# The choice of experts moved from the slots stage into the turns of the first token stage

## The reference, cut to what matters

```python
logits = x @ gate_weight.T
probs = jax.nn.softmax(logits.astype(jnp.float32), axis=-1)
topw, topi = jax.lax.top_k(probs, TOP_K)          # TOP_K = 8 of E = 32
topw = topw / topw.sum(-1, keepdims=True)
...
oh = jax.nn.one_hot(flat_e, E, dtype=jnp.int32)
pos = (jnp.cumsum(oh, axis=0) * oh).sum(-1) - 1   # place of each token in its expert's buffer
buf = jnp.zeros((E, CAPACITY, H), x.dtype).at[flat_e, pos].set(flat_x, mode='drop')
```

## Time and profile before

| | us |
|---|---|
| median of 3 timed runs | 3384.29 |
| the profiled execution, its own time | 3380.68 |
| its span | 3378.9 |
| TensorE busy | 3197.8 (95%) |
| Vector busy | 2735.5 (81%) |
| GpSimd busy | 2081.7 (62%) |
| ACT busy | 1560.9 (46%) |

### The profile page before, as it was taken

One profiled execution on the slowest core, in us unless ns is written; L12 is line 12 of the kernel. 1 busy time (PEld: TensorE's weight loads), 2 busy tenths in 40 slices (PEclk: granted clock), 3 DMA queues, 4 the chain that ended last, 5 costly groups with the idle time before them and its releaser, 6 DMA issues. The chain is left out here.

```text
span 3378.9 us, 55655 instructions
## 1 busy us (share of the span) xinstructions
PE 3197.8 (95%) x17324; PEld 2506.5 (74%) x17324; DVE 2735.5 (81%) x5290; ACT 1560.9 (46%) x5449; POOL 2081.7 (62%) x2335
## 2 busy tenths in 40 slices
PE   7999999999979999999999699999999969999998
PEld 5677777777648888888888577777777757778886
DVE  4788888888677887888887379999999879967775
ACT  1766767667521111111111377777777745321111
POOL 1776666766536777777777477777777753443333
PEclk8999999999979999999999899999999989999999
DMA  7345454454465667676766544555554457730111
GB/s 218 100 137 173 122 166 140 137 174 125 141 174 154 171 169 175 170 166 166 176 164 156 112 128 133 160 163 143 151 172 135 138 164 286 274 103 13 26 13 25
DMA packets 284781, 490.97 MB, mean 145 GB/s; under 512 B 54018, under 2 KB 74818, under 8 KB 283778
## 3 DMA queue, kind: packets, MB, share of 16 engines
q1 hardware_dynamic: 243698, 408.87, 39.6%
q0 software_dynamic: 32256, 77.65, 12.4%
q10 hardware_dynamic: 8592, 1.57, 0.3%
HBM read 250.32 MB, written 136.96 MB: 115 GB/s over the span
## 5 line engine op out<-in xcount | busy, mean ns | idle before, releaser
L915 ACT ACTIVATE c_pr<-ps,t_negmax 128x154 f32<-128x154 f32 x1024 | 385.7, 393 | 180.8 <-DVE t_negmax L684 178.6
L684 DVE TENSOR_REDUCE t_negmax<-ps 128x4 f32<-128x616 f32 x512 | 403.6, 788 | 53.3 <-PE ps L980 52.6
L915 ACT ACTIVATE t_pr<-ps,t_negmax 128x154 f32<-128x154 f32 x1024 | 385.6, 393 | 105.8 <-DVE t_negmax L684 101.4
L707 DVE COPY t_pTm<-ps 128x512 f32<-128x512 f32 x448 | 306.0, 683 | 127.3 <-PE ps L993 123.0
L609 POOL TENSOR_TENSOR t_pr<-t_pr,t_inv 128x512 f32<-128x512 f32 x256 | 275.7, 1077 | 191.0 <-DVE t_inv L699 189.3
L609 POOL TENSOR_TENSOR c_pr<-c_pr,t_inv 128x512 f32<-128x512 f32 x256 | 272.0, 1063 | 196.4 <-DVE t_inv L699 195.0
L980 PE MATMUL ps<-t_kst,t_stack 98*128 98x154 f32 x2048 | 353.0, 291 | 26.3 <-DMA t_stack<-t_q_low 10.1
L980 PEld LDWEIGHTS ps<-t_kst,t_stack 98*128 98x128 f32 x2048 | 279.6, 194 | 38.9 <-issue 17.8
L81 PE MATMUL ps<-e_xT_high,e_wgu_high 128*128 128x512 f32 x768 | 302.4, 394 | 1.4 <-DVE e_xT_low L1508 1.4
L83 PE MATMUL ps<-e_xT_high,e_wgu_low 128*128 128x512 f32 x768 | 299.6, 390 | 0.0
L82 PE MATMUL ps<-e_xT_low,e_wgu_high 128*128 128x512 f32 x768 | 299.4, 390 | 0.0
(11 more groups left out here) (373 smaller groups left out, 9320.9 us busy)
## 6 DMA issues: line engine op xcount, KB each, us to landing
t_stack<-t_q_high SPq DMA_DIRECT2D x1016, 64.0 KB, 2.0
c_wgu_in<-in_gate_upT SPq DMA_DIRECT2D x32, 1536.0 KB, 6.4
t_stack<-t_q_low SPq DMA_DIRECT2D x512, 64.0 KB, 2.0
x_dram<-c_wide_rows SPq DMA_DIRECT2D x32, 1024.0 KB, 7.8
c_wd_in<-in_downT SPq DMA_DIRECT2D x32, 768.0 KB, 4.5
t_xbo<-in_x SPq DMA_DIRECT2D x16, 1024.0 KB, 7.0
xw_dram<-t_z SPq DMA_DIRECT2D x16, 1024.0 KB, 5.3
t_xbo<-x_dram SPq DMA_DIRECT2D x16, 1024.0 KB, 11.0
```

The source lines that it names most:

```text
L684: dve.tensor_reduce(negmax[:, u, :], flat[:, at:at + HG * APART].rearrange("p (h n) -> p h n", h=HG)[:, :, 0:KEYS], AX, ALU.max, negate=Tr ...
L707: dve.tensor_copy(pTm[:, g % 2, :, t * P:(t + 1) * P], ps[:, 4, :].rearrange("p (h n) -> p h n", h=HG)).then_inc(s["pTm"], 1)
L915: op = act.activation(pr[:, u % 4, h, :], flat[:, col:col + KEYS], ACT.Exp, bias=negmax[:, u, h:h + 1], accum_out=total[:, u, h:h + 1])
```

## The change

In the first token stage the two copies behind MAX8 go. One turn later four pieces for that tile stand on Vector's list at positions 8, 13, 18 and 26: `mark` (4 match_replace: the eight largest are overwritten), `pick` (logit minus the largest; the selection as "overwritten differs from the logit"), `step` (step_up, the exponentials times the selection, a copy of the last sub-tile's selection) and `weights` (sum, reciprocal, product). ACT takes the exponential at position 15 (`share_out`). SP stores each tile's weights (`store_weights`) between its load of t_xbo and its store of x. The last tile's pieces follow the last turn. The slots stage loses the whole chain and ACT's store of all weights; TensorE's list begins with the 32 counts and puts the two base matmuls between the key products; Vector empties count banks first and adds the value bias last; GpSimd fills the small part of the table early and does its longest memset (BIG) last. SP waits for 12 made tiles, no longer 13.

```diff
-        LOG = 31
+        LOG, WTS, WEX = 31, (8, 13, 18, 26), 15
...
+            def store_weights(j):
+                sp.wait_ge(s["weighted"], j + 1)
+                sp.dma_start(rows(scr["xw"], j)[:, :, D:XW], weight[:]).then_inc(s["w_stored"], 16)
...
+                if 0 <= i - 3:
+                    store_weights(i - 3)
                 if prev:
...
+            def mark(j):
                 dve.wait_ge(s["top"], j + 1)
-                dve.tensor_copy(c["top8"][:, bass.ds(j * TG * TOPK, TG * TOPK)],
-                                top[:].rearrange("p t k -> p (t k)")).then_inc(s["side_out"], 1)
+                for t in range(TG):
+                    op = dve.match_replace(others[:, t, :], top[:, t, :], logit[:, t, :], LOWEST)
+                op.then_inc(s["others"], 1)
+            def pick(j):
+                dve.wait_ge(s["top"], j + 1)
+                dve.tensor_tensor(share[:], logit[:], top[:, :, 0].unsqueeze(2).to_broadcast([P, TG, E]),
+                                  ALU.subtract).then_inc(s["shifted"], 1)
+                dve.wait_ge(s["others"], j + 1)
+                dve.tensor_tensor(sel[:, 1:1 + TG, :], others[:], logit[:], ALU.not_equal).then_inc(s["picked"], 1)
+            def step(j):
+                dve.wait_ge(s["picked"], j + 1)
+                dve.tensor_tensor(c["step_up"][:, TG * j:TG * j + TG, :], sel[:, 1:1 + TG, :], sel[:, 0:TG, :],
+                                  ALU.subtract).then_inc(s["stepped"], 1)
+                dve.wait_ge(s["shared_out"], j + 1)
+                dve.tensor_tensor(share[:], share[:], sel[:, 1:1 + TG, :], ALU.mult).then_inc(s["chosen"], 1)
+                dve.wait_ge(s["stepped"], j + 2)
+                dve.tensor_copy(sel[:, 0, :], sel[:, TG, :]).then_inc(s["carried"], 1)
+            def weights(j):
+                dve.wait_ge(s["chosen"], j + 1)
+                dve.tensor_reduce(wsum[:], share[:], AX, ALU.add).then_inc(s["summed"], 1)
+                dve.wait_ge(s["summed"], j + 1)
+                dve.reciprocal(wsum[:], wsum[:]).then_inc(s["inverted"], 1)
+                dve.wait_ge(s["inverted"], j + 1)
+                reached(dve, s["w_stored"], 16 * j)
+                dve.tensor_tensor(weight[:], share[:], wsum[:].unsqueeze(2).to_broadcast([P, TG, E]),
+                                  ALU.mult).then_inc(s["weighted"], 1)
             def dot(j, t):
...
+                    if gate and 0 <= j - 1:
+                        for when, piece in zip(WTS, (mark, pick, step, weights)):
+                            if at == when:
+                                piece(j - 1)
...
             unrolled(turn)
+            if gate:
+                for piece in (mark, pick, step, weights):
+                    piece(NG - 1)
...
+            def share_out(j):
+                act.wait_ge(s["shifted"], j + 1)
+                act.activation(share[:], share[:], ACT.Exp).then_inc(s["shared_out"], 1)
...
                         part_out(j)
+                    if at == WEX and gate and 0 <= j - 1:
+                        share_out(j - 1)
...
+            assert n_made[0] == TRI_MADE
+            made(pool.memset(table[:, :, P:LOOK], 0.0))
             made(pool.iota(ramp[:], [[1, NT + 1]], base=0, channel_multiplier=-1, allow_small_or_imprecise_dtypes=True))
...
-            made(pool.memset(table[:, :, P:LOOK], 0.0))
             made(pool.memset(zero[:], 0.0))
+            assert n_made[0] == ZERO_MADE
             made(pool.memset(table[NT:NT + 1, :, 0:P], BIG))
             assert n_made[0] == MADE
...
-            act.wait_ge(s["shifted"], 1)
-            act.activation(prob[:], prob[:], ACT.Exp).then_inc(s["exped"], 1)
-            act.activation(edge[:], edge[:], ACT.Exp).then_inc(s["exped"], 1)
+            for q in range(1, 8, 2):
...
                 act.copy(k["high"][:, two, n, :], k["kf"][:, j % 4]).then_inc(s["khigh"], 1)
-            act.wait_ge(s["weights"], 1)
-            act.dma_start(scr["xw"][0:NTOK, D:XW].rearrange("(t p) e -> p t e", p=P),
-                          prob[:]).then_inc(s["put"], 16)
...
-            logits = c["logits"][:].rearrange("p (t e) -> p t e", e=E)
-            top8 = c["top8"][:].rearrange("p (t k) -> p t k", k=TOPK)
-            link(dve.tensor_tensor(edge[:], top8[:, :, TOPK - 1], top8[:, :, 0], ALU.subtract))
-            dve.tensor_tensor(prob[:], logits, top8[:, :, 0].unsqueeze(2).to_broadcast([P, NT, E]),
-                              ALU.subtract).then_inc(s["shifted"], 1)
-            link(dve.memset(restart[:], 1.0))
-            link(dve.memset(restart[:, :, 0:1], 0.0))
...
             dve.wait_ge(s["falls_mm"], 1)
             dve.tensor_copy(table[:, :, P + 2:LOOK].rearrange("t e w -> t w e"),
                             ps[0:NT + 1, HB + 1, 0:2 * E].rearrange("t (w e) -> t w e", e=E)).then_inc(s["tabled"], 1)
+            dve.wait_ge(s["wv_in"], 32)
+            for n in range(KV_JOBS - 8):
+                value_out(n)
...
-                if e == HB * 4:
-                    pe.wait_ge(s["valued"], KV_JOBS - 8)
-                mm = pe.matmul(ps[0:NT, (HB + e // 4) % 8, (e % 4) * P:(e % 4 + 1) * P], step_up[:, :, e], tri[:],
...
+                mm = pe.matmul(ps[0:NT, (HB + e // 4) % 8, (e % 4) * P:(e % 4 + 1) * P], c["step_up"][:, :, e], tri[:],
                                start=True, stop=True)
                 if e % 4 == 3:
...
+                if j < HB:
+                    return (s["counted1"], 3 + j // 2) if j % 2 else (s["counted0"], 3 + j // 2)
+                return (s["evacuated"], j - HB + 1) if j < 8 + HB else (s["valued"], j - HB - 7)
+            def bases_between(j):
+                if j == 2:
+                    pe.wait_ge(s["made"], TABLE_MADE)
+                    pe.wait_ge(s["counted0"], 4)
+                    pe.wait_ge(s["counted1"], 4)
+                    pe.matmul(ps[0:NT + 1, HB, 0:E], ramp_b[:], table[0:NT, :, P - 1], start=True,
+                              stop=True).then_inc(s["based"], 1)
+                if j == 4:
+                    pe.wait_ge(s["parted"], 1)
+                    pe.matmul(ps[0:NT + 1, HB + 1, 0:2 * E], falls[:], parts[:].rearrange("t w e -> t (w e)"), start=True,
+                              stop=True).then_inc(s["falls_mm"], 1)
+            kv_products(pe, ps, k, s, HB, bank_free, c["key_weights_in"], c["context_in"], bases_between)
```

More of the change, by code:

```diff
@@ L177, with kv_products @@
 KV_JOBS = 13
-def kv_products(pe, ps, k, s, banks, freed, wk_in, ctx_in):
+def kv_products(pe, ps, k, s, banks, freed, wk_in, ctx_in, between=None):
     pe.wait_ge(wk_in, 16)
@@ L185, in kv_products @@
         bank = j % banks
-        if j >= banks:
-            pe.wait_ge(*freed(j - banks))
+        if between:
+            between(j)
+        if freed(j):
+            pe.wait_ge(*freed(j))
         if j == 8:
@@ L738, in logits @@
                 dve.wait_ge(s["side_mm"], j + 1)
[L739 removed]
+                reached(dve, s["picked"], j)
                 dve.tensor_reduce(logit[:], ps[:, T_BANK, :].rearrange("p (t k e) -> p t e k", k=DC, e=E),
@@ L1150, in expert_slots_phase @@
         bkt = sb("bkt", [P, DC, B])
[L1151 to L1154, removed]
         ones, tri = sb("ones", [P, P]), sb("tri", [P, P], BF16)
@@ L1163, in expert_slots_phase @@
         s = Sems(nc, ctx, "r", "wv_in tau_in tail scaled kf khigh matmul evacuated lowered valued stored "
-                               "made shifted exped step weights selected stepped count_mm counted0 counted1 based parted "
+                               "made step count_mm counted0 counted1 based parted "
                                "falls_mm tabled put")
         block = ctx.enter_context(nc.Block())
-        MADE = 13
+        TRI_MADE, TABLE_MADE, ZERO_MADE, MADE = 3, 9, 12, 13
         @block.sync
@@ L1248, in _ @@
                 act.copy(k["high"][:, two, n, :], k["kf"][:, j % 4]).then_inc(s["khigh"], 1)
-            act.wait_ge(s["weights"], 1)
-            act.dma_start(scr["xw"][0:NTOK, D:XW].rearrange("(t p) e -> p t e", p=P),
-                          prob[:]).then_inc(s["put"], 16)
-            for q in range(1, 8, 2):
-                act.wait_ge(s["count_mm"], q + 1)
-                act.copy(table[0:NT, 4 * q:4 * q + 4, 0:P], ps[0:NT, (HB + q) % 8, :].rearrange("t (e n) -> t e n", n=P)).then_inc(
-                    s["counted1"], 1)
         @block.vector
@@ L1307, in _ @@
-            value_out(1)
-            link(dve.reciprocal(ws[:], ws[:]))
-            dve.tensor_tensor(prob[:], prob[:], by_tile(ws), ALU.mult).then_inc(s["weights"], 1)
-            value_out(2)
-            dve.wait_ge(s["made"], MADE)
-            link(dve.memset(table[:, :, P:P + 1], float(P)))
-            link(dve.memset(table[0:1, :, P:P + 1], 0.0))
-            link(dve.memset(table[NT:NT + 1, :, P + 1:P + 2], 1.0))
-            value_out(3)
-            value_out(4)
             for q in range(0, 8, 2):
@@ L1320, in _ @@
```

(13 more changed lines are left out.)

57 lines of the change are left out of this document (21 added, 36 removed).

## The result

| | before | after |
|---|---|---|
| median of 7 timed runs | 3384.29 us | 3393.60 us |
| their range | 3379.73 to 3387.03 | 3388.51 to 3400.38 |
| profiled execution, own time | 3380.68 | 3391.85 |
| its span | 3378.9 | 3390.1 |

The ratio is 1.0031 with a 95% interval of 1.0021 to 1.0041: slower, on the side of the forecast, but 9.3 us between the medians and 11.2 between the profiled executions against the 21 worked out. The forecast median was 3404 us.

What follows compares the result with a forecast made beforehand. TensorE was taken to bound the token stage, with Vector feeding it with little to spare mid-turn. Terms 24.3 + 5.1 - 8.1 gave +21 us, 3402 by the profiled execution, stated as 3404 us; range 3375 to 3414, the forecast's own 3392 to 3414.

Steps and rivals of the forecast that it cites:

- slots stage: Slots stage: 54.7 us shrinks to 46.6, -8.1 (-11 to -4), as value additions no longer queue behind the selection on Vector.
- stage's end: End of first token stage: last tile's pieces, ACT's exponential and an uncovered 64 KB store add 5.1 us (3.5 to 7).
- mechanism: Mid-turn: Vector instructions with two SBUF inputs and GpSimd's SBUF reads take turns, so TensorE waits; token stage +24 us.
- Rival B: Token-stage turns: GpSimd's next instruction doesn't get between two of Vector's; stage +2, total -1, 3383 us by median; chance 0.25.
- Rival C: Turns: nothing costs anything, the copies' 0.43 is kept, slots stage gives 11; total -13, 3371 us; chance 0.15.
- Rival D: Turns: mark waits for GpSimd too and pick pays 2.3 us; stage +39, total +36, 3420 us; chance 0.10.

Runs made afterwards that it cites:

- pick_reduce: Changed kernel with the two two-operand comparisons as one-operand maxima, choice of experts left out: turn 52.78 us, one time of 3379.22 us.
- both_reduce: As pick_reduce, with the three instructions of the step also made one-operand maxima: turn 52.18 us, one time of 3374.53 us.
- carry_reduce: Changed kernel with only the small copy of the last row of choices done as a reduction: turn 53.30 us, one time of 3387.48 us.
- moved: Changed kernel with mark and pick at position 26, step and weights a turn later at 16 and 18, two weight buffers: 3368.18 us, ratio to before 0.9956.
- moved_last_hidden: As moved, with the slots order of counts_last and the last weights store waited for in the slots stage: 3366.51 us, ratio to before 0.9951.
- counts_last: Changed kernel with the slots stage's order undone, key and value products first, counts behind: 3392.27 us, ratio to before 1.0033.

## Why the prediction was right, and what it mis-sized

| term, us | worked out | measured | from |
|---|---|---|---|
| copies out, a turn | -0.43 | -0.68 | table of TensorE's offsets |
| mark | +0.3 | +0.27 | same |
| pick | +1.3 | +1.18 | same; pick_reduce 1.12 |
| step | +0.8 | +0.60 | same; both_reduce and carry_reduce 0.60 |
| weights, exponential, store | 0 | 0 | same; moved |
| up to the first logits | 0 | +0.9 | before any piece has run |
| token stage | +24 | +17 | first to last logits, 16.8 |
| stage's end | +5.1 | +4.4 | 2.6 to 7.0 |
| slots stage | -8.1 | -9.3 | 54.7 to 45.5 |
| sum | +21 | +12.8 | start of the expert stage |

**The mechanism held, the size did not.** Every term of the sum was worked out too slow, and the measured 3393.60 us lies near the lower end of the forecast's own range (3392 to 3414), which was wide enough for that. Pick's two instructions take turns with q_low and xbo; their ends lie 0.15 us behind the ends of q_low and xbo, where 0.15 and 0.2 were worked out, L775 and L778 together take 1.7 us, and the new wait of TensorE stands where it was looked for, at 0.94 us. The weights and the stores are free. Rival B, in which GpSimd doesn't get between the two, gave a turn like that of before; xbo does get between them, and pick_reduce shows what that is worth. Rival C, in which nothing in the turn costs anything, was wrong at these places and came true in the turns of moved. Rival D fell with the mark: MATCH_REPLACE8 takes 0.17 us in the turns, its MATCH_VALUE_LOAD 0.08, with 0.16 us from one pair to the next. In the changed kernel GpSimd has nothing to do at that moment; moved shows the same length beside it:

```profile
527.78 1.13 POOL L628 TENSOR_TENSOR c_pr<-c_pr,t_inv 128x512 f32<-128x512 f32 x1 [1.41 <-DVE t_inv L719]
...
528.32 0.17 DVE L772 MATCH_REPLACE8 t_others<-t_top,t_logit 128x32 f32<-128x32 f32 x1
```

**Copies, mis-sized by 0.25 us a turn.** I summed the two waits that the table named, 0.18 and 0.24. Beside the first, the trace of before has on the weight loads of the same transposes, once in every turn, a third that I passed over, since it names no releaser:

```profile
492.25 0.42 PEld L992 LDWEIGHTS ps<-ident,c_pr 128*128 128x128 f32 x4 [0.59 <-issue]
493.41 0.19 PEld L980 LDWEIGHTS ps<-t_kst,t_stack 98*128 98x128 f32 x1 [0.24 <-ACT c_pr L915]
```

Both idle times are absent at this place of after. By the matmuls' starts the first two, at one place, were worth 0.35 us (4.10 against 3.75 after the logits' reduction) and the one for c_pr with what follows it 0.33, together 0.68, which is nearly the 0.69 that the copies took on Vector. Here Vector fed TensorE without slack, and what it saved came through whole.

**Step, nearly the right size by a partly wrong reason.** I let the two-operand instructions and the copy queue for GpSimd alike and got 0.8. carry_reduce shows that the copy alone makes the 0.60.

**Over the stage** the four differences make 13 x (0.25 + 0.03 + 0.2) + 12 x 0.12 = 7.7 us; between +24.3 and +16.8 lie 7.5.

**The stage's end.** Its terms add up to 5.2, not 5.1. The last store costs less than the 2.4 put on it: 0.4 to issue and 1.4 for the landing, by moved_last_hidden. Vector's list grew by 2.3 us, where 2.4 were worked out.

**Slots stage, nearly the right size by a wrong cost.** The counts were put at 5.6 us, since TensorE starts at the 1.2 GHz level, and took 3.79, so they were over 4.7 us from the stage's start, not 6.6. Behind them it was 35.8 us to the last value addition, where 34.0 + 0.55 were worked out, and 5.0, not 5.4, to the next stage. The first 16 key products paid the lower level instead (5.58 us against 4.41 for the next 16). In moved, in the same order, these 16 took 4.41 at a granted 1.00, which is 1.2 us less and nearly all by which its slots stage is shorter. The reason given for the gain stands: counts_last, with the old order, still has no selection on Vector and reaches it. The order added nothing.

**The total.** 3402 + 3.6 is 3406, not 3404. The working missed by 12 us and the forecast by 10.

## What to carry to other kernels

Where a piece stands on Vector decides what it costs: the same instructions cost 2.05 us a turn, of which 1.78 by pick and step, at places without a gap beside GpSimd, and nothing at places with idle behind them; the changed kernel, 0.3% slower, became 0.4% faster than before by other places and a second buffer for the weights. Cost an inserted instruction that reads two operands in SBUF, or a copy within SBUF, by GpSimd's time line beside it, not by its length, and give a small copy in SBUF another form, such as a reduction, where GpSimd is busy. Where a chain and an order are changed together, undo the order alone before crediting it.

## What the runs showed that was not expected

- The 32 count matmuls of 128x128 in bf16 took 3.79 us at a granted clock of 0.50, the 1.2 GHz level, and 3.76 at 1.00, the 2.4 GHz level (counts_last): some 0.12 us each at both. The clock by stretch, two rows of the changed kernel and one of counts_last:

```profile
core 0: us, PE busy (x), PEclk, DMA share, GB/s
971.60:975.30 3.70, 3.70 (x32) 0.50 0.73 182
975.40:980.80 5.40, 5.40 (x16) 0.79 0.99 335
...
1004.10:1007.90 3.80, 3.79 (x33) 1.00 0.50 99
```

  Before its counts TensorE had been idle for 8.02 us; the 0.79 is the mean of a stretch that starts at 0.50 and ends at 1.00. Each count has its own weights, and both the weight loads and the matmuls start 0.11 us apart at either level. What sets that distance in place of the clock stays open.
- A copy of 32 bf16 elements a partition took 1.26 us in the mean beside GpSimd and 0.17 alone.
- A wait of SP for a store's landing, 4.7 to 6.2 us, went unseen in eight turns of eleven and cost 4.0 to 6.3 us in the three others.
